# Attention in a four-layer conv/SSM/attention kernel: the second score pair of a key step goes behind the values of the last step

## The chip, the cores and the metric

One core of one Trainium2 chip runs the whole kernel. The time is the device time of one execution in microseconds; the kernel before takes 5579.34 us (median of 3 runs, 5577.0 to 5589.4).

## What is computed

Eight samples of 256 channels by 32 x 32 positions (1024 tokens) go through four residual layers with a group norm ahead of each: a selective-scan layer, a multi-head attention, a dilated depthwise convolution and a second multi-head attention with layer norms. The change touches the attention alone, which both attention layers share. Cut to that, the reference is:

```python
q, k, v = qkv[:, :, 0], qkv[:, :, 1], qkv[:, :, 2]           # (b, 1024, 8 heads, 32)
scores = jnp.einsum('bthe,bThe->bhtT', q, k) / jnp.sqrt(32.)
attn = jax.nn.softmax(scores, axis=-1)
out = jnp.einsum('bhtT,bThe->bthe', attn, v)
```

All is float32. There are 16 attentions in an execution (8 samples, layers 1 and 3).

## The kernel before

The kernel is written per engine: each engine has its own program, and semaphores join them. Each engine works in the order in which its program issues. So the order of TensorE's matmuls is the order of the calls in its `attention` function.

An attention is cut into four **phases**: two groups of four heads (`GROUPS`) by two chunks of 512 queries (`NC`). Each phase runs over eight **key steps** (`KT`), one for each 128 keys. A key step has these parts:

- **Score pairs** (L1334). For each of the four heads of the group, TensorE multiplies 128 keys with the 512 queries into one PSUM bank, banks 2 to 5. Two heads are a pair. A pair is issued when ScalarE has read the same banks in the last key step (`p_sb`). The row maximum, negated, stands in two extra rows of `QS`, so that the subtraction is part of the matmul; `nm_in` says that these rows are there.
- **Exponentials** (L615). ScalarE takes a pair of banks, 1024 columns, in one instruction and writes `PT`, of which there are three buffers.
- **Values** (L1286), the function `values(i, between, turn)`. TensorE multiplies the values with `PT` of the key step before, four heads side by side in the columns of the array, into bank 0. It waits for both exponentials of that step. In steps 4 and 7 a group against ones (L1295) gives the denominators in bank 1; the other steps' `PT` are summed first, by GpSimd (L421, `POOL_SUMS`), in the last phase by VectorE (L997, `DVE_SUMS`). The group at L1305 reads the sum at the end of a phase.
- **Row halves** (L1244), the functions `row_scores` and `next_rows(most)`. The row maxima of the next phase must be known before it starts, so TensorE also computes its scores in the other orientation, 128 queries by 512 keys. There are 16 such rows a phase in two halves each, 32 halves. A half goes to bank 6 or 7 in turn, and VectorE reduces it to its maximum (L945). A half waits until VectorE has read the bank's last content, which is the half two before (`r_max`).

`HALF_ROWS` = (5, 4, 4, 4, 5, 5, 5, 0) says how many halves go in each of the eight key steps. `next_rows(most)` issues up to `most` of those that are left for the step. The last phase has no row halves, as no phase follows. In key step 7 `values` also transposes the maxima (`turn_max`, L1249); ScalarE and VectorE make the negated maxima of it (L591, L956), and SP moves them into `QS` (L301). Between the values and what follows, `values` calls `between`: with 1 where a ones group follows, with 2 in the other steps.

In the first key step of a phase the values of the last phase's step 7 go first, then the two score pairs; ScalarE works out the reciprocal denominators (L596, L600), and VectorE normalizes (L964, L966) ahead of the fifth maximum. Before an attention's phases, 32 halves of its first phase are computed among the projections.

Of the kernel before, what the change touches and what calls it, by code (L numbers as in the profile page):

```python
# [50 lines left out]
PHASES = GROUPS * NC  # L51
HALF_ROWS = (5, 4, 4, 4, 5, 5, 5, 0)
TURN_AT = 7
# [39 lines left out]
def build(nc, x, wpack, vpack, w8, out):  # L93
    with ExitStack() as ctx:
# [959 lines left out]
        def _(pe):  # L1054
# [164 lines left out]
            def attention(b, a, X):  # L1219
# [13 lines left out]
                def row_scores(n, cc):  # L1233

                    ph, j, q = n // PHASE_ROWS, n % PHASE_ROWS // 4, n % 4
                    g, c = divmod(ph, NC)
                    h = GH * g + j
                    if c == 0 and q == 0 and cc == 0:
                        pe.wait_ge(*stackedq[g][j](b, (a + 1) * 48))
                        pe.wait_ge(*stackedk[g][j](b, (a + 1) * 48))  # L1240
                    ahead = 2 if ph == 0 else 1
                    if n % PHASE_ROWS >= ahead:
                        pe.wait_ge(*r_max(b, halves(a, n - ahead, cc) + 1))
                    pe.matmul(PS[:, row_slot(n, cc), :], QS[0:kd, c, h, q * P:q * P + P], KS[0:kd, h, cc * N:cc * N + N],  # L1244
                              start=True, stop=True).then_inc(r_ps.sem, 1)

                def turn_max(ph):
                    pe.wait_ge(*m_both(b, a * PHASES + ph + 1))
                    pe.transpose(PS[0:PHASE_ROWS, 6, 0:P], mboth[:, :], ident[:, :]).then_inc(mt_ps.sem, 1)  # L1249
# [25 lines left out]
                def values(i, between, turn=None):  # L1275

                    ph, kt = divmod(i % (PHASES * KT), KT)
                    g = ph // NC
                    sums = POOL_SUMS if ph < PHASES - 1 else DVE_SUMS
                    direct = [k for k in range(KT) if k not in sums]  # L1280
                    pe.wait_ge(*p_sb(b, 2 * i + 2))
                    if kt == 0 and ph > 0:
                        pe.wait_ge(*o_raw(b, i // KT))
                    for j in range(GH):
                        h = GH * g + j
                        ins = pe.matmul(PS[32 * j:32 * j + 32, 0, :], Vt[:, kt, DH * h:DH * h + DH], PT[:, i % 3, j, :],  # L1286
                                        start=(kt == 0), stop=(kt == KT - 1), skip_group_check=True)
                    if kt not in direct:
                        ins.then_inc(pv_ps.sem, 1)
                    between(1 if kt in direct else 2)  # L1290
                    if turn is not None:
                        turn_max(turn)
                    if kt in direct:
                        for j in range(GH):
                            ins = pe.matmul(PS[32 * j:32 * j + 32, 1, :], ones32[:, :], PT[:, i % 3, j, :],  # L1295
                                            start=(kt == direct[0]), stop=False, skip_group_check=True)
                        if kt == KT - 1:
                            between(1)

                            if ph < PHASES - 1:  # L1300
                                pe.wait_ge(*sum_pool(b, pool_sums(a, ph, len(POOL_SUMS) - 1)))
                            else:
                                pe.wait_ge(*sum_dve(b, dve_sums(a, len(DVE_SUMS) - 1)))
                            for j in range(GH):
                                ins = pe.matmul(PS[32 * j:32 * j + 32, 1, :], ones32[:, :], acc[:, ph % 2, j, :],  # L1305
                                                start=False, stop=True, skip_group_check=True)
                        ins.then_inc(pv_ps.sem, 1)

                for ph in range(PHASES):
                    g, c = divmod(ph, NC)  # L1310
                    row = [NC * PHASE_ROWS * (ph + 1), 0]

                    def next_rows(most):
                        for _ in range(min(most, row[1]) if ph < PHASES - 1 else 0):
                            if row[0] % (NC * PHASE_ROWS) == 0:
                                pe.wait_ge(*nm_rest(b, PHASES * a + ph + 1))
                            row_scores(*divmod(row[0], NC))
                            row[0], row[1] = row[0] + 1, row[1] - 1

                    for kt in range(KT):  # L1320
                        i = key_step(a, ph, kt)
                        row[1] = HALF_ROWS[kt]
                        if kt == 0:
                            if ph > 0:
                                values(i - 1, next_rows)
                            else:
                                next_rows(NC)
                            pe.wait_ge(*nm_in(b, 32 * (PHASES * a + ph + 1)))
                        for pr in range(2):
                            if ph + kt > 0:  # L1330
                                pe.wait_ge(*p_sb(b, 2 * i - 2 + pr + 1))
                            for jj in range(2):
                                h = GH * g + 2 * pr + jj
                                ins = pe.matmul(PS[:, 2 + 2 * pr + jj, :], KS[:, h, kt * P:kt * P + P], QS[:, c, h, :],  # L1334
                                                start=True, stop=True)
                            ins.then_inc(s_ps.sem, 1)
                            next_rows(1)
                        if kt > 0:
                            values(i - 1, next_rows, ph + 1 if kt == TURN_AT and ph < PHASES - 1 else None)
                        next_rows(row[1])  # L1340
                values(key_step(a, PHASES - 1, KT - 1), lambda most: None)

# [38 lines left out]
            for b in range(B):  # L1381
                block0(b)
                group_norm(b, 1)
                attention(b, 0, xg)
                pe.wait_ge(*o_sb(b, 4))
                project(b, 0, oT)
                group_norm(b, 2)
                block2(b)
                group_norm(b, 3)
                chan_norm(b, 0, xg)  # L1390
                attention(b, 1, xg)
                pe.wait_ge(*o_sb(b, 8))
                chan_norm(b, 1, oT)
                norm_means(b, 4)
                project(b, 1, oT, lambda: norm_variances(b, 4))
                pe.wait_ge(*gn_xa(b, 5))
                pe.wait_ge(*gn_xb(b, 5))
                pe.wait_ge(*x_new(b, 16))
# [12 lines left out]
def key_step(a, ph, kt):  # L1411

    return (PHASES * a + ph) * KT + kt


def pool_sums(a, ph, k):

    return ((PHASES - 1) * a + ph) * (len(POOL_SUMS) - 1) + k


def dve_sums(a, k):

    return (len(DVE_SUMS) - 1) * a + k
# [95 lines left out]
```

## Time and profile before

| | |
|---|---|
| median of 3 runs | 5579.34 us |
| profiled execution: time, span | 5587.96 us, 5586.2 us |
| TensorE busy (matmul) | 4255.3 us, 76% |
| VectorE busy | 3701.3 us, 66% |
| ScalarE busy | 2100.0 us, 38% |
| GpSimd busy | 2111.3 us, 38% |
| mean granted TensorE clock | 0.848 of full speed |
| DMA, mean | 23 GB/s |

The program repeats for eight samples, some 693 us each. Busy time is the time in which an engine executes an instruction; a TensorE that is busy isn't TensorE at its peak, as its matmuls are pipelined and their ends are modelled. "PEld" is its weight loads, which run beside matmuls. In the rows further down, a line such as L1244 is the line of the kernel that issued the instruction, `x4` is how many like instructions were merged, and an arrow names what ended the idle time before it. In a table of stretches a row has: stretch, length, then busy time (and count) of PE, PEld, DVE, ACT and POOL, then the granted clock, the DMA share and GB/s. Each matmul of values, ones and sums is executed as two, so a group of four heads shows as x8.

### The profile page before, as it was taken

The page shows a single profiled execution, that of the slowest core. Times are in us where ns is not written, and L with a number is a line of the kernel's source. Part 1 is how long each engine was busy: PE and PEld are TensorE (multiplying, and loading weights), DVE is VectorE, ACT ScalarE, POOL GpSimd, SP SyncE. Part 2 cuts the span into 40 slices and gives each one's busy share as a digit, 9 for nine tenths or more (in the row PEclk, how much of TensorE's full clock was granted, in tenths as well). Part 3 has the DMA queues.
Part 4 walks back from the last instruction along what each step waited for, and adds up shares of the span by engine and source line. Part 5 has one row for each costly group of instructions (what it writes and reads, how often), then busy time and mean ns, then how long its engine had stood idle before and what let it go on. Part 6 is the DMA issues. An engine that isn't in the chain of part 4 may idle for free.

```text
span 5586.2 us, 44537 instructions
## 1 busy us (share of the span) xinstructions
PE 4255.3 (76%) x16298; PEld 1848.8 (33%) x16298; DVE 3701.3 (66%) x4825; ACT 2100.0 (38%) x2575; POOL 2111.3 (38%) x713
## 2 busy tenths in 40 slices
PE   4688866888668886688866888668886697866978
PEld 2233422333224332243322433224332243322433
DVE  7863677637776368763687646876468664686746
ACT  3233442334423354233442435324253242532425
POOL 4531435404354044440444404444045340453404
PEclk7689976999779997698976999779897798977989
DMA  0020100210002100021000220001200012000120
GB/s 35 0 54 18 29 8 0 54 26 21 8 3 51 32 15 8 8 46 38 9 8 8 46 46 1 8 13 42 45 1 8 21 33 46 1 8 21 26 46 9
DMA packets 62957, 125.76 MB, mean 23 GB/s; under 512 B 18825, under 2 KB 21001, under 8 KB 62482
## 3 DMA queue, kind: packets, MB, share of 16 engines
q1 hardware_dynamic: 62738, 122.91, 9.5%
q8 instruction: 129, 2.11, 0.2%
q14 instruction: 90, 0.74, 0.0%
HBM read 12.23 MB, written 8.39 MB: 4 GB/s over the span
## 4 chain that ended last, share of the span: by engine, by line
PE 46%; DVE 29%; issue 10%; ACT 7%; SPq 4%; POOL 2%; DMA 1%; DVEq 0%; ACTq 0%; POOLq 0%
DVE mx L945 9%; PE PS L1244 8%; PE PS L1286 8%; PE PS L1078 7%; PE PS L1334 6%; PE PS L1368 4%; DVE work L837 3%; DVE work L839 3%; PE PS L1137 3%; ACT PT L615 2%; PE PS L1178 2%; SPq L284 2%; PE PS L1295 2%; SPq L293 2%; DVE dstk L777 1%
## 5 line engine op out<-in xcount | busy, mean ns | idle before, releaser
L945 DVE TENSOR_REDUCE mx<-PS 128x1 f32<-128x512 f32 x2048 | 1337.0, 686 | 426.0 <-PE PS L1244 421.2
L615 ACT ACTIVATE PT<-PS 128x1024 f32<-128x1024 f32 x1024 | 1006.1, 1022 | 692.6 <-PE PS L1334 663.1
L421 POOL TENSOR_TENSOR piece<-PT 128x2048 f32<-128x2048 f32 x48 | 220.0, 4582 | 2188.1 <-ACT PT L615 2188.1
L1244 PE MATMUL PS<-KS,QS 96*128 96x512 f32 x2048 | 896.6, 480 | 194.6 <-DMA KS<-piece 84.5
L421 POOL TENSOR_TENSOR piece<-piece,PT 128x2048 f32<-128x2048 f32 x192 | 877.6, 4571 | 59.8 <-ACT PT L615 48.6
L401 POOL TENSOR_TENSOR work<-work,Crep 128x1024 f32<-128x1024 f32 x256 | 615.8, 2407 | 439.2 <-DVE work L837 241.2
L1334 PE MATMUL PS<-QS,KS 98*128 98x512 f32 x2048 | 682.0, 425 | 46.1 <-DMA QS<-nm 21.9
L1244 PEld LDWEIGHTS PS<-KS,QS 96*128 96x128 f32 x2048 | 378.8, 198 | 815.4 <-DVE mx L945 574.6
L1286 PE MATMUL PS<-PT,Vt 128*32 128x512 f32 x4096 | 547.0, 606 | 27.4 <-ACT PT L615 27.4
L1178 PE MATMUL PS<-dstk,sel 128*128 128x512 f32 (+1 forms) x640 | 316.8, 570 | 320.9 <-DVE work L839 129.9
L1178 PE MATMUL PS<-ustk,sel 128*128 128x512 f32 (+1 forms) x640 | 333.9, 595 | 280.3 <-DVE work L822 152.5
L533 ACT ACTIVATE PS<-PS,Aneg 128x1024 f32<-128x1024 f32 x256 | 278.3, 1087 | 696.3 <-PE PS L1178 595.5
L1334 PEld LDWEIGHTS PS<-QS,KS 98*128 98x128 f32 x2048 | 377.1, 197 | 291.4 <-ACT PT L615 164.8
L1078 PE MATMUL PS<-xg,W 128*128 128x512 f32 x640 | 355.2, 711 | 45.1 <-ACT xg L447 20.4
L1178 PEld LDWEIGHTS PS<-ustk,sel 128*128 128x128 f32 x640 | 139.7, 257 | 595.3 <-issue 275.4
L1178 PEld LDWEIGHTS PS<-dstk,sel 128*128 128x128 f32 x640 | 153.0, 269 | 459.3 <-DVE work L837 182.5
L1137 PE MATMUL PS<-work,ysel 128*32 128x512 f32 (+1 forms) x1536 | 273.6, 803 | 40.1 <-POOL work L405 30.6
L822 DVE TENSOR_TENSOR work<-PS,Brep 128x1024 f32<-128x1024 f32 (+1 forms) x256 | 250.3, 978 | 71.0 <-PE PS L1178 67.8
L937 DVE SCALAR_TENSOR_TENSOR piece<-PS,V,piece 128x1024 fp32r<-128x1024 f32 x64 | 82.1, 1283 | 279.6 <-ACT piece L579 279.6
L405 POOL TENSOR_TENSOR work<-work,Crep 128x640 f32<-128x640 f32 x128 | 210.1, 1644 | 138.7 <-DVE work L848 80.1
L1030 DVE TENSOR_TENSOR xr<-xr,rl 128x512 f32<-128x512 f32 x32 | 22.1, 692 | 319.3 <-ACT rl L638 319.3
L380 POOL TENSOR_TENSOR work<-work 128x1024 f32<-128x1024 f32 x16 | 42.1, 2632 | 477.3 <-ACT work L497 477.3
(211 smaller groups left out, 5261.0 us busy)
## 6 DMA issues: line engine op xcount, KB each, us to landing
QS<-piece SPq DMA_DIRECT2D x384, 128.0 KB, 2.4
KS<-piece SPq DMA_DIRECT2D x384, 128.0 KB, 2.4
xin<-x SPq DMA_DIRECT2D x8, 1024.0 KB
out<-xr SPq DMA_DIRECT2D x8, 1024.0 KB, 4.0
W<-wpack SPq DMA_DIRECT2D x2, 1024.0 KB
QS<-nm SPq DMA_DIRECT2D x128, 8.0 KB, 1.9
W<-wpack SPq DMA_DIRECT2D x1, 576.0 KB
W<-wpack SPq DMA_DIRECT2D x2, 256.0 KB
```

Source lines behind the costliest of these rows:

```text
L401: pool.tensor_tensor(slot, h, Crep[:, at:at + L], ALU.mult).then_inc(hC_sb.sem, 1)
L421: pool.tensor_tensor(total, first, PT[:, i % 3, :, :], ALU.add).then_inc(sum_pool.sem, 1)
L533: act.activation(dst, src, ACT.Exp, scale=Aneg[:, ps * SG + g:ps * SG + g + 1]).then_inc(dA_sb.sem, 1)
L615: act.activation(PT[:, i % 3, 2 * pr:2 * pr + 2, :], PS[:, 2 + 2 * pr:4 + 2 * pr, :], ACT.Exp, scale=SCALE).then_inc(p_sb.sem, 1)
L822: dve.tensor_tensor(dBx_slot(n)[:, 0:w], src, Brep[:, at:at + w], ALU.mult).then_inc(dBx_sb.sem, 1)
L945: dve.tensor_reduce(mx[:, at, cc:cc + 1], PS[:, row_slot(n, cc), :], AX.X, ALU.max).then_inc(r_max.sem, 1)
L1078: ins = pe.matmul(PS[:, bank, :], w[:, k, m * P:m * P + P], X[:, k, c * N:c * N + N], start=(k == 0), stop=(k == CT - 1))
L1137: ins = pe.matmul(PS[32 * j:32 * j + 32, c, 0:N if ps < 2 else W3], ysel[:, q % 4, :], src, start=(q % 4 == 0), stop=(q % 4 == 3), skip_gr ...
L1178: ins = pe.matmul(PS[:, slot + c, 0:wc], sel[:, g % 8, :], stk[:, g // 8, at + c * N:at + c * N + wc], start=True, stop=True)
L1244: pe.matmul(PS[:, row_slot(n, cc), :], QS[0:kd, c, h, q * P:q * P + P], KS[0:kd, h, cc * N:cc * N + N], start=True, stop=True).then_inc(r_ ...
L1286: ins = pe.matmul(PS[32 * j:32 * j + 32, 0, :], Vt[:, kt, DH * h:DH * h + DH], PT[:, i % 3, j, :], start=(kt == 0), stop=(kt == KT - 1), s ...
L1334: ins = pe.matmul(PS[:, 2 + 2 * pr + jj, :], KS[:, h, kt * P:kt * P + P], QS[:, c, h, :], start=True, stop=True)
```

## The change

In a key step of before TensorE issues: score pair 0, one half, score pair 1, one half, values of the last step with two halves (one, where the ones group follows), and what is left of the step's halves. After the change it issues: score pair 0, two halves, values of the last step (with one half between the values and the ones group, where there is one, and none otherwise), score pair 1, two halves, and what is left. In key step 0 the values of the last step stay ahead of both pairs, as before. In key step 7 the transpose, which is part of `values`, comes ahead of score pair 1 too.

```diff
--- before.py
+++ after.py
@@ -1334,9 +1334,9 @@
                                 ins = pe.matmul(PS[:, 2 + 2 * pr + jj, :], KS[:, h, kt * P:kt * P + P], QS[:, c, h, :],
                                                 start=True, stop=True)
                             ins.then_inc(s_ps.sem, 1)
-                            next_rows(1)
-                        if kt > 0:
-                            values(i - 1, next_rows, ph + 1 if kt == TURN_AT and ph < PHASES - 1 else None)
+                            next_rows(2)
+                            if pr == 0 and kt > 0:
+                                values(i - 1, lambda most: next_rows(1) if most == 1 else None, ph + 1 if kt == TURN_AT and ph < PHASES - 1 else None)
                         next_rows(row[1])
                 values(key_step(a, PHASES - 1, KT - 1), lambda most: None)
```

The two numbers in `next_rows` and the place of the call are the whole change; no instruction, buffer or wait is new.

## Rows read from the trace of the kernel before

**Rows 1.** The page, part 5: line engine op out<-in xcount | busy, mean ns | idle before.
```profile
L945 DVE TENSOR_REDUCE mx<-PS 128x1 f32<-128x512 f32 x2048 | 1337.0, 686 | 426.0 <-PE PS L1244 421.2
```

**Rows 2.** Stretches: one phase with row halves and the last, without. Columns: section above.
```profile
3149.20:3182.20 33.00, 30.78 (x157) 12.69 (x153) 22.91 (x37) 16.99 (x19) 22.86 (x5) 1.00 0.00 1
...
3215.00:3238.00 23.00, 19.44 (x112) 6.25 (x110) 15.54 (x9) 17.32 (x20) 0.00 (x0) 1.00 0.00 1
```

**Rows 3.** Chain of waits (start us, us, what): one step of four row halves.
```profile
3128.03 0.99 PE PS L1286 x8
3129.03 0.45 PE PS L1244
...
3129.49 0.70 DVE mx L945
...
3130.24 0.50 PE PS L1244
3130.74 0.46 PE PS L1334 x2
3131.20 0.23 PE PS L1244
```

**Rows 4.** Timeline (start, length, engine, operation, [idle before <- releaser]) of that step.
```profile
3129.49 2.67 DVE L945 TENSOR_REDUCE mx<-PS 128x1 f32<-128x512 f32 x4 [0.73 <-PE PS L1244]
...
3130.24 0.19 PEld L1244 LDWEIGHTS PS<-KS,QS 96*128 96x128 f32 x1 [0.52 <-DVE mx L945]
...
3130.28 1.99 ACT L615 ACTIVATE PT<-PS 128x1024 f32<-128x1024 f32 x2 [1.43 <-PE PS L1334]
```

**Rows 5.** Chain of waits: values groups that open and close the phase's longer steps.
```profile
3131.43 0.99 PE PS L1286 x8
...
3135.56 0.99 PE PS L1286 x8
...
3140.40 0.99 PE PS L1286 x8
```

**Rows 6.** Timeline of the turn of a phase (step 7).
```profile
3143.96 1.06 PE L1286 MATMUL PS<-PT,Vt 128*32 128x512 f32 x8
...
3144.96 0.28 PE L1249 MATMUL PS<-ident,mboth 128*16 128x128 f32 x1
...
3145.66 1.06 PE L1286 MATMUL PS<-PT,Vt 128*32 128x512 f32 x8 [0.43 <-ACT PT L615]
```

**Rows 7.** Timeline: GpSimd's last two sums, and the first step of the next phase.
```profile
3136.81 9.19 POOL L421 TENSOR_TENSOR piece<-piece,PT 128x2048 f32<-128x2048 f32 x2 [0.72 <-ACT PT L615]
...
3151.85 0.68 DVE L964 TENSOR_TENSOR oT<-PS,lr 128x512 f32<-128x512 f32 x1
...
3153.70 0.50 PE L1244 MATMUL PS<-KS,QS 96*128 96x512 f32 x1 [0.18 <-DVE mx L945]
```

**Rows 8.** Timeline of the last phase, which has no row halves.
```profile
3215.64 3.85 ACT L615 ACTIVATE PT<-PS 128x1024 f32<-128x1024 f32 x4
...
3217.61 0.74 PE L1334 MATMUL PS<-QS,KS 98*128 98x512 f32 x2 [0.18 <-ACT PT L615]
...
3218.28 1.07 PE L1286 MATMUL PS<-PT,Vt 128*32 128x512 f32 x8
...
3222.14 11.60 DVE L997 TENSOR_TENSOR piece<-piece,PT 128x2048 f32<-128x2048 f32 x5 [0.26 <-ACT PT L615]
...
3233.24 1.06 PE L1286 MATMUL PS<-PT,Vt 128*32 128x512 f32 x8 [0.42 <-ACT PT L615]
```

**Rows 9.** Timeline, VectorE: L964 after the third and the last phase, this attention.
```profile
3215.76 0.69 DVE L964 TENSOR_TENSOR oT<-PS,lr 128x512 f32<-128x512 f32 x1 [3.75 <-ACT lr L600]
...
3237.38 0.69 DVE L964 TENSOR_TENSOR oT<-PS,lr 128x512 f32<-128x512 f32 x1 [3.65 <-ACT lr L600]
```

**Rows 10.** The same two points in the next attention.
```profile
3458.87 0.69 DVE L964 TENSOR_TENSOR oT<-PS,lr 128x512 f32<-128x512 f32 x1 [3.75 <-ACT lr L600]
...
3482.01 0.69 DVE L964 TENSOR_TENSOR oT<-PS,lr 128x512 f32<-128x512 f32 x1 [3.83 <-ACT lr L600]
```


## The prediction

> **What bounds the kernel now.** I read the page first, then the stretches by phase, then the chain of waits with the timeline of one key step beside it. The change touches only the attention loop, so the question is what ends last in a key step there. By the stretches TensorE is busy 30.8 of 33.0 us in a phase with row halves, at a granted clock of 1.00, and 19.4 of 23.0 us in the last phase [rows 2]; that looks like TensorE as the bound with nothing to gain or lose from an order. The chain shows a loop of two engines instead. From one group of values to the next it reads [rows 3, 5]: values 0.99, row half 0.45, VectorE's maximum of that half 0.70, the row half that reuses its bank 0.50, two scores 0.46, row half 0.23, values: 3.40 us. VectorE is idle in the same step: 0.73 us before four maxima in a row that take 2.67, or 0.67 each [rows 4]; over the kernel it waits 421 us for row halves [rows 1]. ScalarE waits 1.43 us per step for scores and isn't near the bound [rows 4].
>
> From these rows come the prices used below. TensorE: a matmul of 512 columns that follows another costs 0.235 us (0.46 for two); the first after values 0.44; a row half that had to wait for a maximum ends 0.50 after its weight load is released, of which the load is 0.19 [rows 3, 4], and the release comes 0.04 after the maximum (3129.49+0.70 to 3130.24). Values cost 1.00. VectorE: a maximum after a pause ends 0.72 after its half, one in a row 0.67. The rule of the banks: half k may start when the maximum of half k-2 is over.
>
> Set values at 0 and call the halves behind them C, D, those before the next values A, B. Before: values end 1.00, C 1.44, D 1.68, scores 2.15; maximum of C 2.16, so A ends 2.70; scores 3.17; the maximum of D was over at 2.83, under the scores, so B ends 3.41. That is the 3.40 measured. The same sums give 4.12 for values 3 to 4 and 4.85 for values 4 to 5 (with the ones group), where the rows have 4.13 and 4.84 [rows 5].
>
> **The change, part by part.** No instruction is added or removed; no DMA or SP work moves. In steps 1 to 7 the values of the last step, with the ones group and the transpose of the turn where there is one, go ahead of the second score pair.
> (1) Steps with four halves, three a phase, from values 0 to values 3. Values end 1.00, the score pair now behind them 1.68, C 1.92, D 2.15; maximum of C 2.64, of D 3.31; the first score pair ends 2.62; A is released at 2.68 and ends 3.18; B has no scores in front of it any more, waits for the maximum of D, is released at 3.35 and ends 3.85. So 3.85 for 3.41: +0.44, three times +1.32. VectorE's pause grows: it finishes A and B at 0.80 of the next step and gets C only at 1.92.
> (2) Values 3 to 4 (five halves): C 1.92, D 2.15, E 3.18, scores 3.65, the next half 3.89, the last half waits for E's maximum (3.98) and ends 4.52: +0.40. Values 4 to 5: values 1.00, half 1.44, ones 2.44, scores 3.12, halves 3.36 and 3.60, their maxima 4.08 and 4.75, scores 4.07, halves 4.62 and 5.29: 5.29 for 4.85, +0.44.
> (3) Values 5 to 6: three halves then scores, 3.65 for 3.64 by the same sums, +0.
> (4) Turn, values 6 to 7: now 1.70 us, since both exponentials were started before values 6 [rows 6]. After: values and transpose 1.28, score pair 0.47, 0.09 to the exponential, 1.00 for it (two take 1.99 [rows 4]), 0.04 to release values 7: 2.89, +1.19. The negated maxima and their DMAs come behind that exponential and beside values 7 as now, so nothing more is late there.
> (5) Values 7 to the next phase's values 0: unchanged, +0. The order there ends with a half that waits for VectorE's last maximum behind the normalization: 3151.85, and the half released at 3153.70 [rows 7]. I get the same instant with the new order, since that maximum starts from the third half, which still ends right behind the first scores.
> What hides beside: GpSimd's last two sums end 9.2 us after they start, at 3146.0, and the group that reads them starts some 2.9 us behind values 7, at 3148.6 [rows 6, 7]. The sums would start later in their phase, after the late exponentials, and end by my sums 1.3 us before they are needed; without that cover each phase would pay the excess.
> A phase with halves: 1.32+0.40+0.44+1.19 = 3.35 us longer. There are 48 (three in each of 16 attentions): 161 us.
> (6) The last phase. Four exponentials run 3215.64 to 3219.49, 0.96 each, so the second ends at 3217.57; values 7 start at 3233.24, 15.6 us later, 2.23 a step [rows 8]. There TensorE puts the scores of both pairs in while ScalarE works. After, values wait for the second exponential of the last step, and the second scores stand behind them: 0.04 release, 1.00 values, 0.73 the score pair after a change (0.74 [rows 8]), 0.09, exponential 1.00 = 2.86 a step. Seven steps: 20.0 for 15.6, +4.4. VectorE's sums (2.32 each [rows 8]) then fit in with room. Sixteen times 4.4: 70 us.
> (7) At each attention's start one score pair moves behind the first values, which come that much sooner: -0.7 (the same 0.74), in all -11.
> Sum: 161+70-11 = 220 us. The profiled execution spans 5586.2 us and took 5587.96, 8.6 more than the median of 5579.34, so 5808 against it and 5799 against the median.
>
> Not shown by any row of before is a step with two waits of row halves in a row. The second may cost its whole 0.50 as the first does, or only the 0.235 of a half that follows at once; I take 0.50, because the released half of rows 3 also comes straight behind other matmuls (by the sums 0.05 us behind the scores). At the other end steps (1) and (2) lose 0.26 each, 1.3 a phase, 62 us in all: 5737.
> A page of the Trainium skill speaks to this (TensorE: Matmul & The Clock Gate, "Step-by-step: what each phase is for"): TensorE draws weight loads ahead of matmuls in flight. If a waiting half's load were drawn ahead too, the chain would be 0.19 shorter at each second wait; five of them in 48 phases make 46 us, 5753. The load itself stands idle 0.52 us for the maximum [rows 4], so this case's trace doesn't agree where the load has a wait of its own.
>
> **The rivals.**
> Only the bank wait is misjudged: the maximum of D is over in time for B in some way, B ends 3.42, and the row steps stay as they are. For it: before, just this wait is hidden. Against: it was hidden by the scores that are moved away. Then only (4), (6), (7) count: 57+70-11 = +116, 5695.
> The last phase keeps its pace, because VectorE's sums (2.32 a step) and not the exponentials set it: +150, 5729. Against: 2.86 is a chain of TensorE and ScalarE alone.
> The other side: TensorE's own work is the bound and the waits cost it no restart, as the busy share suggests to whoever stops at the stretches. A step of four halves is then 8 matmuls, 1.90, and values 1.20 = 3.10, a gain of 0.31, thrice 0.93; 0.73 in values 3 to 4 (there VectorE's five maxima are the floor), 0.29 in 4 to 5, 0.70 in 5 to 6; the turn costs 1.15: -1.50 a phase, -72. The last phase's chain without restarts is 1.00+0.47+0.97 = 2.44, +24; with -12 at the starts -60 in all: 5519. It decides once a maximum with both hand-overs fits into what stands between a half and the one that reuses its bank; that is 0.95 us of work for A, where the maximum takes 0.72 and the restart 0.54. So it needs the restart under 0.23.
> The clock falls. The last phase of this attention takes 21.6 us from normalization to normalization [rows 9], that of the next 23.1 [rows 10]. That phase has a stretch at the lower level (1.2 GHz), so one costs 1.5 us. With more idle time per step such stretches could come in each of the 64 phases: +99, 5898. For it: the lower busy share; against: rows 2, where 84% busy still had 1.00. The Trainium skill (same page, "A second HAM failure mode: psum-queue depth-cycling") says that small frequent pauses between groups that cycle through PSUM banks can make the clock swing; it is the same case as this rival, and phases with halves, full of such pauses, show 1.00 here.
> That the change doesn't do what it says: where values don't follow a score pair (step 0) the code path is the old one; I have counted that, so no own case.
>
> **How the numbers follow.** Forecast 5799, chance 0.74 with its own range 5735 to 5840; clock 0.12 (5898); row steps as before 0.06 (5695); last phase as before 0.05 (5729); TensorE alone 0.03 (5519). The range 5725 to 5900 takes in the forecast, the clock case and the last-phase case, and leaves the rest out with what a mis-sized term may add. A measurement of this kernel can tell about 0.2% from no change. Slower holds all but the last case and an unseen remainder: 0.95; same 0.02; faster 0.03.
>
> **What would show it.** Steps of four halves at 3.85 us from values to values; VectorE's idle time before the four maxima at 1.1 to 1.2 and the group's waits for row halves up by over 100 us; the turn at 2.9; the last phase at 2.86 a step, its exponentials single with some 1.8 us between pairs; granted clock in those phases still 1.00. Wrong it would be if the step stays near 3.4 (then the bank wait is hidden after all), if the turn doesn't grow (something else was late there), or if the clock of those stretches drops.

## The result: 5806.7 us, 4.0% slower

The changed kernel takes 5806.7 us (median of 4 runs, 5800.3 to 5813.8) for 5578.2 us before ("X for Y" means X now, where Y stood in the kernel compared with): 1.040 times as long, 95% interval 1.0387 to 1.0413. The forecast was 5799, the range 5725 to 5900. Its profiled execution took 5809.63 us and spans 5807.9. No engine has more instructions. Busy are TensorE 4324.5 us (69 more), VectorE 3675.8 (26 less), ScalarE 2124.0 (24 more). What grew most is waiting. The page of the changed kernel, part 5 (busy, mean ns | idle before it and for whom), against [rows 1]:

```profile
L945 DVE TENSOR_REDUCE mx<-PS 128x1 f32<-128x512 f32 x2048 | 1310.0, 686 | 567.0 <-PE PS L1244 566.2
L615 ACT ACTIVATE PT<-PS 128x1024 f32<-128x1024 f32 x1024 | 1028.8, 1022 | 894.4 <-PE PS L1334 847.2
```

VectorE waits 566 us for row halves, 145 more than before; ScalarE waits 847 us for score pairs, 184 more than the 663 on the page of before.

By stretches (the columns of [rows 2]): a phase with halves and the last phase.

```profile
3306.90:3341.00 34.10, 29.96 (x149) 12.07 (x148) 19.76 (x34) 16.71 (x20) 22.81 (x5) 1.00 0.01 1
3341.00:3367.00 26.00, 18.41 (x108) 6.41 (x108) 15.05 (x9) 16.64 (x18) 0.00 (x0) 1.00 0.00 1
```

These stretches, like those of [rows 2], are cut by hand and don't measure a phase: the first covers 34.1 of its phase's 35.8 us, and the last phase takes 25.9 us from normalization to normalization, for 21.6 in [rows 9]. The granted clock is 1.00 in both.

The chain of waits of the changed kernel, in steps of four halves, with the values that open the longer steps:

```profile
3243.77 1.00 PE PS L1286 x8
3244.77 0.66 PE PS L1334 x2
3245.42 0.25 PE PS L1244
...
3245.70 1.30 DVE mx L945 x2
...
3247.04 0.50 PE PS L1244
3247.54 0.99 PE PS L1286 x8
...
3251.99 0.99 PE PS L1286 x8
...
3257.20 0.99 PE PS L1286 x8
```

From values to values: 3.77 us, for 3.40 in [rows 3, 5]. In the place of one maximum of 0.70 there now stand two, 1.30: the last half ahead of the values waits for the second maximum. Values 3 to 4 take 4.45 us and values 4 to 5 5.21.

VectorE's side of the same step (timeline; [rows 4] have 2.67 and 0.73), and the weight load of the second half that waits:

```profile
3245.70 2.57 DVE L945 TENSOR_REDUCE mx<-PS 128x1 f32<-128x512 f32 x4 [1.19 <-PE PS L1244]
...
3247.04 0.19 PEld L1244 LDWEIGHTS PS<-KS,QS 96*128 96x128 f32 x1 [0.41 <-DVE mx L945]
```

The turn, step 7 (timeline; [rows 6] answer to it). Values 6, then the exponential of the second pair by itself, then values 7, for which TensorE stands idle 1.11 us:

```profile
3260.76 1.06 PE L1286 MATMUL PS<-PT,Vt 128*32 128x512 f32 x8
...
3262.54 1.02 ACT L615 ACTIVATE PT<-PS 128x1024 f32<-128x1024 f32 x1 [0.59 <-PE PS L1334]
...
3263.62 1.07 PE L1286 MATMUL PS<-PT,Vt 128*32 128x512 f32 x8 [1.11 <-ACT PT L615]
```

2.86 us for 1.70. And the last phase, two groups of values with ScalarE between them (against [rows 8]):

```profile
3345.65 1.06 PE L1286 MATMUL PS<-PT,Vt 128*32 128x512 f32 x8 [0.65 <-ACT PT L615]
...
3347.41 1.94 ACT L615 ACTIVATE PT<-PS 128x1024 f32<-128x1024 f32 x2 [0.90 <-PE PS L1334]
...
3348.49 1.06 PE L1286 MATMUL PS<-PT,Vt 128*32 128x512 f32 x8 [0.65 <-ACT PT L615]
```

2.84 us a step for 2.23. The exponentials come two in a row, 1.94 us, the second of one step and the first of the next, with ScalarE idle 0.90 us between.

### The profile page after: what moved, and what is told of

It reads as the page before. It is cut to its first block, busy times and chain, and to the rows that moved or that the text cites. A ratio compares the mean times of both kernels' runs of the same rounds, so it can differ in the third digit from the quotient of the medians.

```text
span 5807.9 us, 44537 instructions
## 1 busy us (share of the span) xinstructions
PE 4324.5 (74%) x16298; PEld 1860.8 (32%) x16298; DVE 3675.8 (63%) x4825; ACT 2124.0 (37%) x2575; POOL 2108.3 (36%) x713
## 4 chain that ended last, share of the span: by engine, by line
PE 44%; DVE 31%; issue 9%; ACT 7%; SPq 4%; POOL 2%; DMA 2%; DVEq 0%; ACTq 0%; POOLq 0%
DVE mx L945 12%; PE PS L1286 9%; PE PS L1334 7%; PE PS L1078 6%; PE PS L1244 6%; PE PS L1368 4%; ACT PT L615 3%; DVE work L837 3%; DVE work L839 3%; PE PS L1137 2%; PE PS L1178 2%; SPq L284 2%; SPq L293 2%; PE PS L1295 2%; DVE dstk L777 1%
## 5 line engine op out<-in xcount | busy, mean ns | idle before, releaser
L945 DVE TENSOR_REDUCE mx<-PS 128x1 f32<-128x512 f32 x2048 | 1310.0, 686 | 567.0 <-PE PS L1244 566.2
L615 ACT ACTIVATE PT<-PS 128x1024 f32<-128x1024 f32 x1024 | 1028.8, 1022 | 894.4 <-PE PS L1334 847.2
L1244 PE MATMUL PS<-KS,QS 96*128 96x512 f32 x2048 | 882.9, 477 | 238.9 <-DVE mx L945 89.9
L1334 PE MATMUL PS<-QS,KS 98*128 98x512 f32 x2048 | 714.2, 440 | 45.8 <-DMA QS<-nm 24.4
L1286 PE MATMUL PS<-PT,Vt 128*32 128x512 f32 x4096 | 561.1, 621 | 135.9 <-ACT PT L615 135.9
L1244 PEld LDWEIGHTS PS<-KS,QS 96*128 96x128 f32 x2048 | 403.9, 199 | 711.2 <-DVE mx L945 462.6
L1334 PEld LDWEIGHTS PS<-QS,KS 98*128 98x128 f32 x2048 | 360.0, 198 | 505.3 <-issue 243.0
L1368 PE MATMUL PS<-xg,DW 128*64 128x512 f32 (+11 forms) x1056 | 212.8, 532 | 18.1 <-ACT xg L447 18.1
```

The costliest lines, as they stand in the source:

```text
L615: act.activation(PT[:, i % 3, 2 * pr:2 * pr + 2, :], PS[:, 2 + 2 * pr:4 + 2 * pr, :], ACT.Exp, scale=SCALE).then_inc(p_sb.sem, 1)
L945: dve.tensor_reduce(mx[:, at, cc:cc + 1], PS[:, row_slot(n, cc), :], AX.X, ALU.max).then_inc(r_max.sem, 1)
L1368: ins = pe.matmul(dst, DW[:, t, ky * 3 + kx, 64 * hh:64 * hh + 64], src, start=first, stop=last, skip_group_check=True)
```

## Where the 222 us are

The maxima of a phase are gathered at L952 and the output is normalized at L964, so the starts of these two cut an attention into its phases. These are the three L952 of the attention shown:

```profile
3261.13 0.19 DVE L952 TENSOR_REDUCE mboth<-mx 128x16 f32<-128x32 f32 x1
...
3298.32 0.19 DVE L952 TENSOR_REDUCE mboth<-mx 128x16 f32<-128x32 f32 x1
...
3334.14 0.19 DVE L952 TENSOR_REDUCE mboth<-mx 128x16 f32<-128x32 f32 x1
```

Summed over the 16 attentions, from one such point to the next. A middle phase holds the turn of the phase ahead of it; the first phase holds no turn:

| part of an attention | before, us | after, us | difference | of before, each | of after, each |
|---|---|---|---|---|---|
| first phase (L952 to L952) | 514.2 | 547.7 | +33.5 | 31.5 to 34.9 | 33.5 to 35.9 |
| two middle phases | 1055.5 | 1165.8 | +110.3 | 33.0 | 35.8 (19), 37.2 to 37.4 (13) |
| turn into the last phase (L952 to L964) | 95.0 | 109.0 | +14.0 | 5.94 | 6.82 |
| last phase (L964 to L964) | 347.8 | 417.5 | +69.7 | 21.6 to 21.9 (15), 23.1 | 25.9 (13), 26.4 to 27.3 (3) |
| sum | 2012.5 | 2240.0 | +227.5 | | |

That is 227.5 us; the profiled spans differ by 221.7 and the medians by 228.5. The rest of the program, some 3570 us, is 5.8 us shorter than in the profile of before. The change doesn't touch it; over the kernels of this study (those with short maxima aside) it lies between 3550 and 3574 us, so a difference of spans is not to be explained more finely than that.

Of the middle phases' 110.3 us, 32 x 2.84 = 90.9 come from the order and 19.4 from 13 phases that hold a stretch at the lower clock (the first above, 37.19 us at a mean granted clock of 0.95; the next has none, 35.82 us at 1.00). No middle phase of before holds one. The expectations below, which were written with a count of 14, mean these 13. In the rows of TensorE such a stretch begins behind a pause of 0.73 us, one half ahead of values 0: the values take 1.73 us for 1.06, at the lower level (1.2 GHz) for most of that length.

```profile
3271.54 0.50 PE L1244 MATMUL PS<-KS,QS 96*128 96x512 f32 x1 [0.73 <-DVE mx L945]
3271.96 1.73 PE L1286 MATMUL PS<-PT,Vt 128*32 128x512 f32 x8
```

All 13 stretches begin at this place. The pause is 0.72 to 0.97 us there in all 32 middle phases, and 0.18 at most in those of before ([rows 7]): the new order makes it longer. But 19 phases with the same pause keep the clock.

## Experiments

Theory: a row half needs other work of TensorE between it and the half that reuses its bank; the change takes that work away, and separately puts values and a score pair between two exponentials. Rivals: that the late exponential alone costs (at the turn and in the last phase), that VectorE's sums hide the last phase, that the order costs TensorE time whatever VectorE does, and that the loss is mostly clock.

### The change in parts: e1, e2, e3

Each has the new order in some steps only, by a condition in place of the change (against before; each run has one of the first three lines, without the comment, and two removed lines aren't shown):

```diff
+                            early = ph < PHASES - 1 and kt < TURN_AT      # e1
+                            early = ph < PHASES - 1 and kt == TURN_AT     # e2
+                            early = ph == PHASES - 1                      # e3
+                            next_rows(2 if early else 1)
+                            if early and pr == 0 and kt > 0:
+                                values(i - 1, lambda most: next_rows(1) if most == 1 else None, ph + 1 if kt == TURN_AT and ph < PHASES - 1 else None)
+                        if not early and kt > 0:
+                            values(i - 1, next_rows, ph + 1 if kt == TURN_AT and ph < PHASES - 1 else None)
```

**e1.** 

> Only key steps 0 to 6 of the phases with row halves have the new order; the turn (step 7) and the last phase keep the old one. Theory (the bank wait): a step of four halves takes 3.77 us from values to values (3.41 before), a phase without a stretch at the lower clock grows by 1.6 us, 48 phases less 11 us at the attentions' starts: +68 us, 5646. Rival (nearly all of the loss is the late exponential at the turn and in the last phase): within 10 us of before, 5578 to 5590. Rival (the clock): as the theory, but the stretches at the lower clock that the changed kernel has in 14 of its 32 middle phases are here too, +20 us more.

Measured: 5703.3 us, ratio 1.0217 (1.0202 to 1.0233), +121 us. That refutes the first rival: over half of the loss is in the steps. It is also 57 us more than I expected. Its L952:

```profile
3203.25 0.19 DVE L952 TENSOR_REDUCE mboth<-mx 128x16 f32<-128x32 f32 x1
...
3238.35 0.19 DVE L952 TENSOR_REDUCE mboth<-mx 128x16 f32<-128x32 f32 x1
...
3275.03 0.19 DVE L952 TENSOR_REDUCE mboth<-mx 128x16 f32<-128x32 f32 x1
```

A middle phase takes 35.11 us, 2.13 more than before and not 1.6; 36.68 with a stretch at the lower clock, which 4 of the 32 have, not 13, though the pause ahead of values 0 is 0.74 us in all of them here too.

**e2.** 

> Only key step 7 of the phases with row halves has the new order (values and transpose ahead of the second score pair). Theory: values 6 to values 7 takes 2.86 us for 1.70, 48 times 1.16 = +56 us, 5634, and nothing else moves. If the longer pause ahead of values 7 is also what lets the clock fall, the middle phases show stretches at the lower clock and the time is some 20 us more, 5654. Rival (the turn's delay is caught up while VectorE waits anyway, so that it costs nothing): 5578.

Measured: 5632.8 us, ratio 1.0091 (1.0076 to 1.0106), +51 us.

```profile
3191.30 0.19 DVE L952 TENSOR_REDUCE mboth<-mx 128x16 f32<-128x32 f32 x1
...
3224.93 0.18 DVE L952 TENSOR_REDUCE mboth<-mx 128x16 f32<-128x32 f32 x1
```

A middle phase takes 33.65 us, 0.67 more, and not 1.16. Together the two have 2.13+0.67 = 2.80, which is the 2.84 of the whole change. So the sum was right and I had cut it in the wrong place. When the second score pair of step 7 moves behind values 6, it also leaves the stretch between values 5 and values 6. In the changed kernel the pair of step 6 takes that place, so that stretch stays the same; in e2 it gets shorter by one pair (3.18 us for 3.63), and in e1 longer (4.10). That moves 0.5 us in each of 48 phases, some 25 of the 57 us by which e1 is over its expectation; its stretches at the lower clock in middle and last phases cost some 11, and the attentions' starts gained less than the 11 us that I had taken off. The remainder is open. The total of e2 is near its expectation for another reason: in 10 of the 16 last phases there is a stretch at the lower clock (23.2 to 24.7 us for 21.6; 24.7 us over all 16), though the last phase has the order of before, where one of 16 holds one.

**e3.** 

> Only the last phase of each attention, which has no row halves, has the new order. Theory (values and second scores stand between two exponentials): its seven steps go from 2.23 to some 2.85 us, +4.3 us a phase, 16 phases: +69 us, 5647. Rival (VectorE's sums of 2.32 us set that phase's pace and hide it): at most +10 us, 5588.

Measured: 5651.3 us, ratio 1.0124 (1.0109 to 1.0140), +69 us. Every last phase takes 25.88 us for 21.6, the other phases are as before. This term is shown as it was summed. The three parts add up to 241 us, and the whole change costs 228; the clock stretches that come and go between the four kernels are of that size.

### Halves moved, values not: e4

```diff
-                            next_rows(1)
+                            next_rows(2)
                         if kt > 0:
```

> Two row halves behind each score pair as in the changed kernel, but the values stay behind both pairs as before: score pair, two halves, score pair, two halves, values. Theory (a half must have other work of TensorE between it and the half that reuses its bank): the second two halves have only one matmul and one score pair in front of them, so they wait for both maxima; by the sums a step of four halves takes 3.77 us although no values moved, a phase grows by some 1.4 us, the turn and the last phase stay: +65 us, 5643. Rival (it is the place of the values, with the late second exponential, that costs): steps stay at 3.41 us and the time at 5578 to 5590. Rival (pairs of halves are what VectorE likes, fewer pauses): faster than before.

Measured: 5662.9 us, ratio 1.0149 (1.0132 to 1.0166), +81 us. No values and no exponential moved and the kernel is slower all the same. Chain of waits, one step of four halves:

```profile
3191.39 1.00 PE PS L1286 x8
3192.39 0.66 PE PS L1334 x2
3193.05 0.25 PE PS L1244
...
3193.32 1.30 DVE mx L945 x2
...
3194.75 0.47 PE PS L1244
3195.22 1.00 PE PS L1286 x8
```

3.83 us from values to values (the next one takes 3.79), by the sums 3.77, with the same pair of maxima of 1.30 as in the changed kernel. A middle phase without a stretch at the lower clock grows by 1.2 to 1.4 us, as forecast. The time is above the forecast because of such stretches: 10 of the 32 middle phases and 11 of the 16 last ones hold one. The turn (5.94 us) and the order of the last phase are untouched. So two halves in a row, with too little between them and the next user of their banks, cost as much as the whole change does in such a step.

### Shorter maxima: e5, e6

```diff
-                    dve.tensor_reduce(mx[:, at, cc:cc + 1], PS[:, row_slot(n, cc), :], AX.X,
+                    dve.tensor_reduce(mx[:, at, cc:cc + 1], PS[:, row_slot(n, cc), 0:N // 2], AX.X,
```

**e5**, the kernel before with it. 

> The kernel before, with VectorE's maximum of a half over 256 of its 512 columns (the softmax is then shifted by less than the true maximum; TensorE's work is the same). From 686 ns for 512 columns and 190 for the 32 of mboth I estimate 0.42 us for it. Both theories: a step of four halves comes down from 3.41 to 3.13 us, near TensorE's own 3.10, and the kernel to some 5480. What counts is the difference to the next run.

**e6**, the changed kernel with it. 

> The changed kernel with the same short maxima. Theory (the bank wait): with shorter maxima the two halves ahead of the values wait less; a step of four halves takes 3.26 us, 0.13 above the run before instead of 0.36, while the turn and the last phase lose what they lost. So the difference to the run before shrinks from 226 us to some 140: about 5620. Rival (the order itself costs TensorE time, whatever VectorE does): the difference stays at 226 us, about 5706.

Measured: 5437.2 and 5588.4 us; the difference is 151 us where it was 228. Clock stretches disturb the totals: 15 of the 16 last phases of e5 hold one, 8 of e6. By the phases without them the difference would be some 165 us (an estimate from their lengths), and a middle phase of e6 takes 1.19 us more than one of e5, where it was 2.84. A step of e5:

```profile
3078.72 0.99 PE PS L1286 x8
...
3081.87 0.99 PE PS L1286 x8
```

and of e6:

```profile
3121.72 1.00 PE PS L1286 x8
3122.72 0.66 PE PS L1334 x2
3123.38 0.46 PE PS L1244 x2
3123.84 0.47 PE PS L1334 x2
3124.30 0.65 PE PS L1244 x2
3124.96 1.00 PE PS L1286 x8
```

3.15 and 3.24 us: of the 0.37 that the new order costs a step, 0.09 is left once a maximum is short. In this step of e6 no maximum stands in the chain any more. In these steps TensorE's order by itself is nearly free; it costs through VectorE's maxima. At the turn and in the last phase the late exponential costs by itself (e2, e3). That the two halves' wait is the cause in such steps I call shown, by e4 and by this pair. The last phase is unchanged by it (25.88 us in the eight of e6 without a stretch at the lower clock), as it has no maxima.

### Which pause brings the clock down: e7, e11

**e7** (against the changed kernel).

```diff
                             ins.then_inc(s_ps.sem, 1)
+                            if pr == 1 and kt == TURN_AT and ph < PHASES - 1:
+                                for _ in range(4):
+                                    pe.matmul(PS[:, 7, :], KS[:, h, 0:P], QS[:, c, h, :], start=True, stop=True)
```

> The changed kernel with four more matmuls of 512 columns in the turn, behind the second score pair of step 7, into bank 7, whose content isn't needed then; nothing reads them. They take some 0.95 of the 1.11 us in which TensorE waits there for the exponential. If that pause is what brings the clock down in 14 of the 32 middle phases (37.3 us for 35.8), those stretches go and the time falls by some 20 us to 5787. Rival (the clock falls for another pause, such as that of VectorE's normalization ahead of values 0): it stays within 8 us of 5806.

Measured: 5810.1 us, against 5806.7 for the changed kernel. The pause at the turn is down to 0.21 us, from 1.11, and 14 of the 32 middle phases hold a stretch all the same (1175.4 us together, for 1165.8 in the changed kernel). The pause at the turn isn't it.

**e11** (against the changed kernel).

```diff
-                            next_rows(2)
+                            if pr == 0 and kt == 1 and 0 < ph < PHASES - 1:
+                                next_rows(1)
+                                for _ in range(3):
+                                    pe.matmul(PS[:, 1, :], KS[:, h, 0:P], QS[:, c, h, :], start=True, stop=True)
+                                next_rows(1)
+                            else:
+                                next_rows(2)
```

> The changed kernel with three more matmuls of 512 columns into bank 1 (free at that point; nothing reads them) in step 1 of the second and third phase, between its two halves ahead of values 0, where TensorE waits 0.73 us for VectorE's maximum behind the normalization. Theory (this pause brings the clock down in 14 of the 32 middle phases): all middle phases take 35.8 us, the time falls by some 20 us to 5787. Rival (not this pause either): within 8 us of 5806.

Measured: 5801.8 us, ratio to before 1.0392 (1.0376 to 1.0408). A pair of L952 of one attention:

```profile
3247.79 0.18 DVE L952 TENSOR_REDUCE mboth<-mx 128x16 f32<-128x32 f32 x1
...
3283.60 0.19 DVE L952 TENSOR_REDUCE mboth<-mx 128x16 f32<-128x32 f32 x1
```

The pause is gone, and all 32 middle phases take 35.8 us, together 1146.5 for 1165.8 in the changed kernel. The pause ahead of values 0, where VectorE normalizes, is what these stretches hang on. But the kernel gained only 5 us: 9 of the 16 last phases now take 27 to 28.6 us, where 3 took 26.4 to 27.3 in the changed kernel; all 16 together 11.6 us more. The first half of my expectation came true and the second did not. What decides whether a given pause in a last phase brings the clock down I didn't settle.

### The other way about: e8, e9, and what beats both

**e8** (against before).

```diff
-                            next_rows(1)
+                            if pr == 1 or kt == 0:
+                                next_rows(1 if kt == 0 else 2)
```

> The other way about: from step 1 on both score pairs, then two halves, then the values with the rest of the halves. Between the halves behind the values and those that reuse their banks now stand both score pairs. Theory (what stands between a half and its bank's next one counts): a step of four halves takes 3.30 us for 3.41, also values 4 to 5 gain 0.11; four such steps in 48 phases, -21 us, 5559 to 5561. Rival (two halves in a row are bad in any place): no gain, 5580 or more.

Measured: 5575.6 us (ten runs, 5560.1 to 5582.2), ratio 0.9986 (0.9976 to 0.9997): a gain of 5 us, where 21 were expected. The chain of waits shows the step as it was summed, 3.30 us:

```profile
3142.38 0.99 PE PS L1286 x8
3143.38 0.66 PE PS L1244 x2
3144.04 0.94 PE PS L1334 x4
3144.97 0.71 PE PS L1244 x2
3145.68 1.00 PE PS L1286 x8
```

The half that waited now has both score pairs in front (x4), and no maximum stands in the chain. All middle phases take 32.5 us, 0.46 less than before. The first and middle phases together gained 24 us, and the last phases lost 24.6: eight of them take 24.6 to 24.9 us, a ninth 23.2. TensorE in one of these, and the stretch behind it:

```profile
3197.39 0.74 PE L1334 MATMUL PS<-QS,KS 98*128 98x512 f32 x2 [0.99 <-ACT PT L615]
3198.30 1.22 PE L1334 MATMUL PS<-QS,KS 98*128 98x512 f32 x2 [0.18 <-ACT PT L615]
...
3198.00:3206.00 8.00, 7.82 (x27) 2.75 (x26) 3.61 (x2) 4.23 (x5) 0.00 (x0) 0.57 0.01 2
```

Behind the pause of 0.99 us, in which ScalarE works on the denominators first, one pair of scores still takes its 0.74 us; the next takes 1.22, where [rows 8] have 0.74 at the same place (3217.61), and the mean granted clock of the 8 us is 0.57. This pause stands in all 16 last phases of e8, and in all 16 of before, whose order there is the same and of which one holds a stretch. So the pause alone doesn't bring the clock down; what else has to come together is open.

**e9** (against before; e8 with more matmuls).

```diff
                             ins.then_inc(s_ps.sem, 1)
-                            next_rows(1)
+                            if ph == PHASES - 1 and kt == 0 and pr == 1:
+                                for _ in range(4):
+                                    pe.matmul(PS[:, 7, :], KS[:, h, 0:P], QS[:, c, h, :], start=True, stop=True)
+                            if pr == 1 or kt == 0:
+                                next_rows(1 if kt == 0 else 2)
```

> The order of e8 (both score pairs, two halves, values, the other halves), and in the last phase's step 0 four more matmuls of 512 columns into bank 7, whose content is no longer needed, behind the second score pair; nothing reads them. In e8 the phases with halves gained 0.46 us each, but the last phase took 24.7 us for 21.6 in 8 of 16 attentions: its matmuls ran at the lower clock right behind the 0.99 us in which TensorE waits there for the first exponential. Theory (that pause brings the clock down): with it filled all last phases take about 21.6 us, the time falls by some 20 us against e8 to 5550 to 5560. Rival (the clock falls there for another reason): last phases of 24.7 us stay and the time is that of e8, 5570 to 5580.

Measured: 5549.5 us (5540.9 to 5556.4), ratio 0.9936 (0.9924 to 0.9949), 34 us below before and 257 below the changed kernel. The pause is full (L1339, x4), and the second pair of scores behind it takes 0.73 us where e8 has 1.22:

```profile
3185.27 1.07 PE L1339 MATMUL PS<-QS,KS 98*128 98x512 f32 x4
...
3187.08 0.73 PE L1334 MATMUL PS<-QS,KS 98*128 98x512 f32 x2 [0.18 <-ACT PT L615]
```

Of the 16 last phases 13 take 21.6 to 21.9 us; the sum is 350.5 us for 372.4 in e8. In the other three (22.4 to 24.0 us; the one shown is among them) the first scores wait 1.17 to 1.56 us for the DMA of the negated maxima, ahead of the filled pause. That the filling is the cause is likely, not shown: before has 15 such last phases without it. The attentions account for 22 of the 34 us; the rest lies outside them, within the spread named above. This is the fastest of these kernels that takes the maxima over whole rows (e5 is faster): it adds work that nobody reads, put where the engine would stand idle.

**e10** is e9, and moves one instruction of VectorE.

```diff
                     dve.tensor_tensor(oT[:, g, cs], PS[:, 0, :], lr[:, 1, :], ALU.mult).then_inc(o_raw.sem, 1)
+
+                def add_bias(ph):
...
                     dve.wait_ge(*o_raw(b, j + 1))
                     dve.tensor_scalar(oT[:, g, cs], oT[:, g, cs], v(bq, 4 + g), None, ALU.add).then_inc(o_sb.sem, 1)
...
                             row_max(*divmod(n, NC))
                             n += 1
+                            if kt == 1 and k == 1 and ph >= 1:
+                                add_bias(ph - 1)
```

> e9, and VectorE adds the bias of the normalized output (L966, 0.49 us) in step 1 behind the second maximum instead of ahead of step 0's last maximum, for which a half and values 0 wait. Theory: 0.49 us in each of the 32 middle phases, -16 us against e9, about 5537. Rival (the gap ahead of values 0 is set by ScalarE's exponentials of step 0, which end only a little earlier): under 5 us.

Measured: 5719.1 us, ratio 1.0242 (1.0228 to 1.0256), 170 us slower than e9. The bias, at its new place (L970 in this kernel), with GpSimd beside it:

```profile
3214.07 4.53 POOL L421 TENSOR_TENSOR piece<-PT 128x2048 f32<-128x2048 f32 x1 [8.58 <-ACT PT L615]
...
3214.33 4.56 DVE L970 TENSOR_SCALAR oT<-oT,V 128x512 f32<-128x512 f32 x1
```

The instruction of 0.49 us takes 4.56 there, and ends 0.3 us after GpSimd's sum beside which it started. Each middle phase loses 5.2 us or more: TensorE waits 3.57 us for the maximum behind the bias, and the values behind that wait take 1.94 us for 1.06. At its old place no GpSimd instruction runs. The Trainium skill (SBUF — State Buffer, "SBUF: two separate sides") says that VectorE in a two-port mode and GpSimd share a port pair by an exclusive lock, held for a whole instruction by whichever starts first, and names `tensor_scalar` among the operations that can enter such a mode (same page, "Who interferes with whom"). The trace agrees with that rule: GpSimd started 0.26 us earlier, and the bias ended just behind it. In which mode the bias ran no trace shows. I hadn't looked at what runs beside the new place.

**e12** (against before).

```diff
                     direct = [k for k in range(KT) if k not in sums]
+                    split = kt not in direct and kt < TURN_AT - 1
...
                         h = GH * g + j
+                        if j == 2 and split:
+                            between(1)
                         ins = pe.matmul(PS[32 * j:32 * j + 32, 0, :], Vt[:, kt, DH * h:DH * h + DH], PT[:, i % 3, j, :],
...
-                    between(1 if kt in direct else 2)
+                    between(1 if kt in direct or split else 2)
```

`split` holds in steps without a ones group whose values belong to steps 0 to 5. 

> The kernel before with one row half in the middle of the values (behind two of the four heads) and the other behind them, in steps whose values have no ones group: score pair, half, score pair, half, two heads, half, two heads, half. Each half then has at least 0.9 us of other work between it and the next of its bank, so by the bank wait no half waits any more, and TensorE's own work sets the step: 3.10 us and 0.20 for the second change to values, 3.30, if two heads cost half of four; 48 phases of some four such steps: -20 us, 5560. Rival (four heads side by side are what makes values cost 1.00, two cost nearly as much): steps of 3.6 us or more, slower by 40 us or more.

Measured: 5754.3 us, ratio 1.0305 (1.0291 to 1.0319). The rival holds. Two heads (x4) and the half behind them:

```profile
3243.56 1.05 PE L1289 MATMUL PS<-PT,Vt 128*32 128x512 f32 x4
...
3244.54 0.50 PE L1244 MATMUL PS<-KS,QS 96*128 96x512 f32 x1
```

0.98 us from the start of two heads to the half, where four heads take 1.00. The next such step starts at 3247.78, 4.22 us later. Spacing the halves ideally is worth nothing at that price.

## Why the prediction was right, and where it was right by luck

- **What bounds a step.** Shown. VectorE's maxima and the reuse of two banks, not TensorE's busy share, set a step with halves: e4 without moved values, e5 and e6 with short maxima.
- **(1) and (2), steps with halves.** Right in mechanism, a little too large: 3.85 forecast and 3.77 measured, 4.52 and 4.45, 5.29 and 5.21. The term at fault is the maximum in a row: 0.67 was taken from the 2.67 of [rows 4], which contain a short wait of VectorE for the last of the four halves (by [rows 3] it ends at 3131.43, and three maxima in a row would be over sooner); in the changed kernel two in a row end 1.30 after the first's start and four 2.57, so one in a row costs 0.60 to 0.63.
- **The second wait in a row**, for which no row of before stood, costs its whole 0.50 (3247.04 in the chain above). Its weight load isn't drawn ahead: it starts at 3247.04 too, 0.04 behind the maximum. The low end of that bound, 5737, is excluded, and with it the 5753.
- **(3) and (4).** The stretch from values 5 to 6 takes 3.64 us for 3.63, and the turn is 2.86 us against 2.89. As a sum right; as a statement about the turn alone wrong, as e2 shows: the pair that moves at the turn costs 0.67 net.
- **(5)** Forecast at no change; values 7 to 0 take 8.34 us for 8.48, mostly because of the same shorter maximum. What the forecast saw as the same instant hid something: TensorE reaches its wait there sooner and stands idle 0.73 us for 0.18, which is where the clock falls. GpSimd's sums end 1.0 us before the group that reads them (3265.47 and 3266.47), where 1.3 was forecast, so nothing had to be paid there. In all a middle phase grows by 2.84 us for the 3.35 forecast.
- **(6)** 2.86 forecast, 2.84 measured; 70 us forecast, 69.7 measured.
- **(7)** Too large. From L952 to values 0 a first phase takes 8.89 us on average for 9.32: 0.43 sooner and not 0.7, some 7 us in all for 11. And in four first phases (one of before) values 0 now run at the lower clock (1.94 us), some 4 us more by the lengths of these phases, an estimate.
- **The clock.** I gave it 0.12 as a rival of its own, all or nothing. It is a part of the result: 13 of 32 middle phases hold a stretch of some 1.5 us, 19.4 us in all. That made up for terms that were too large: for the phases with halves and their turns I had 150 us, and without these stretches they grew by 138. So that 5799 comes so near to 5806.7 is in part luck: the forecast left out one cost, 19 us, and overstated others by 12.
- **Signs to look for.** Steps near 3.85, turn near 2.9, last phase 2.86 and VectorE's waits up by over 100 us all came; its pause before four maxima is 1.19. Single exponentials with 1.8 us between pairs in the last phase didn't come: they are two in a row with 0.90 us idle between, at the forecast length of the step. "Granted clock still 1.00" didn't hold for 13 middle phases.
- **The other rivals.** "Row steps as before" and "last phase as before" are refuted by e1 and e3. "TensorE alone" is refuted by the sign; e6 shows how near it comes once the maxima are short.

## What to carry to other kernels

Where two engines hand small buffers back and forth, write down for each item what stands between it and the next user of its buffer, on both engines. An order that bunches items up costs their waits, even with the same work and a busy share above 90%; an order that puts the longest unrelated work between an item and its buffer's next user (e8) gains in those steps. When an instruction is moved, look at what the other engines do at the new place, as GpSimd in e10, and read its duration there first.

## What I had not expected of the hardware

- Short pauses of TensorE, 0.7 to 1.0 us, inside phases in which it is otherwise busy for 70 to 90% of the time bring its granted clock from 2.4 to 1.2 GHz in some places and not in others with the same code. Such a stretch costs 1.2 to 3.8 us. Matmuls that nobody reads, put into the pause, kept it up in 32 of 32 middle phases (e11), and likely in 13 last phases (e9), but the stretches may turn up at another pause: e11 gave back over half. The unchanged last phase shows how loosely pause and clock hang together: the same 0.99 us pause went with a stretch in one of 16 before and in 9 of 16 in e8.
- VectorE's `tensor_scalar` of 128x512 took 4.56 us for 0.49 beside a GpSimd `tensor_tensor` (e10).
- Values of two heads side by side in the columns of the array take 0.98 us, of four heads 1.00 (e12): what is dropped from such a group is not saved.
